# Gathered messages of a graph layer: 18 slots in groups of three, one-hots with one rounded weight, and the weight's rest added to the low halves

## The reference

```python
def _rgcn_conv(x, src, dst, etype, W, root, b):
    x_src = x[src]
    seg = dst * num_rel + etype
    sums = segment_sum(x_src, seg, num_nodes * num_rel)
    cnt = segment_sum(ones, seg, num_nodes * num_rel)
    mean = (sums / maximum(cnt, 1.0)[:, None]).reshape(num_nodes, num_rel, -1)
    out = einsum('nri,rio->no', mean, W)
    return out + x @ root + b

h = relu(_rgcn_conv(xn, src, dst, etype, W1, root1, b1))
gnn = _rgcn_conv(h, src, dst, etype, W2, root2, b2)
x = x + gnn + mix(xn)          # mix: a linear attention
x = x + ffn(_layernorm(x))     # an attention with routed low-rank parts
```

## Time and profile before

| | us |
|---|---|
| median of 3 runs | 3384.78 |
| lowest and highest run | 3378.73, 3389.24 |
| span of the profiled execution | 3605.0 |
| TensorE busy in it | 3193.7 (89%) |
| VectorE | 1792.2 (50%) |
| ScalarE | 782.7 (22%) |
| GpSimd | 1291.1 (36%) |
| layer 0's gather stage, from the 13th gather (636) to the last take (1174) | 538 |
| layer 1's gather stage (1715.5 to 2257.8) | 542 |

### The profile page before, as it was taken

One profiled execution on the slowest core, in us unless ns is written; L12 is line 12 of the kernel. 1 busy time (PEld: TensorE's weight loads), 2 busy tenths in 40 slices (PEclk: granted clock), 3 DMA queues, 4 the chain that ended last, 5 costly groups with the idle time before them and its releaser, 6 DMA issues.

```text
span 3605.0 us, 61984 instructions
## 1 busy us (share of the span) xinstructions
PE 3193.7 (89%) x19397; PEld 2367.7 (66%) x19398; DVE 1792.2 (50%) x2967; ACT 782.7 (22%) x1113; POOL 1291.1 (36%) x1388
## 2 busy tenths in 40 slices
PE   6999999887787799999878878999987899998999
PEld 5788887665665688887666666676755555555555
DVE  6566666444444433333444544334367764556451
ACT  2211211000000312122000000444421345434540
POOL 2681112556555000001555555000042246533652
PEclk9999999989998999999988998999998899999999
DMA  4343344667677133233667767300032000000003
GB/s 142 104 135 118 115 143 132 225 227 251 225 229 232 50 105 113 97 113 115 228 214 237 243 228 227 108 13 26 13 107 70 19 18 18 1 18 18 18 13 104
DMA packets 101161, 433.83 MB, mean 120 GB/s; under 512 B 19648, under 2 KB 19971, under 8 KB 96818
## 3 DMA queue, kind: packets, MB, share of 16 engines
q0 software_dynamic: 55712, 266.87, 22.9%
q1 hardware_dynamic: 42593, 124.83, 11.0%
q10 hardware_dynamic: 2736, 40.50, 3.1%
HBM read 355.21 MB, written 76.88 MB: 120 GB/s over the span
## 4 chain that ended last, share of the span: by engine, by line
PE 64%; DVE 12%; DVEq 7%; issue 7%; another core or an unknown queue 6%; ACT 2%; POOL 1%; DMA 0%; POOLq 0%; ACTq 0%; SPq 0%
PE PS L1574 24%; PE PS L1704 12%; PE PS L1918 5%; PE PS L1737 3%; PE PS L1583 3%; PE PS L1849 2%; DVE NM L1495 2%; DVE HOT L1241 2%; DVEq L1241 2%; PE PS L1745 2%; PE PS L1901 2%; PE PS L1782 1%; PE PS L1902 1%; PE PS L1766 1%
## 5 line engine op out<-in xcount | busy, mean ns | idle before, releaser
L1574 PE MATMUL PS<-WHL,XT 128*125 (+1 forms) x3240 | 553.1, 330 | 13.3 <-DVE WHL L1002 4.2
L1574 PE MATMUL PS<-WHL,HT 128*125 (+1 forms) x3240 | 534.8, 327 | 8.6 <-DVE ROOT L1200 8.6
L1574 PEld LDWEIGHTS PS<-WHL,XT 128*125 128x125 f16 (+1 forms) x3240 | 442.0, 138 | 100.4 <-issue 12.4
L1574 PEld LDWEIGHTS PS<-WHL,HT 128*125 (+1 forms) x3240 | 443.1, 137 | 94.1 <-DVE ROOT L1200 9.0
L1223 DVE SCALAR_TENSOR_TENSOR ROOT<-PS,GS,ROOT x182 | 185.3, 1018 | 523.9 <-remote 257.4
L646 POOL TENSOR_TENSOR PL<-PF 125x500 bf16<-125x500 f32 (+1 forms) x360 | 322.3, 928 | 248.9 <-ACT PF L859 248.2
L1704 PE MATMUL PS<-GATB,HOT 128*125 128x384 f16 x1440 | 285.5, 358 | 94.7 <-DVE HOT L1241 68.3
L1241 DVE SCALAR_TENSOR_TENSOR HOT<-NODE,DSTF,WHLO (+1 forms) x720 | 297.4, 475 | 78.6 <-issue 69.7
L1084 DVE SCALAR_TENSOR_TENSOR MSG<-PS,MSG 125x768 f16<-125x768 f32 x160 | 153.0, 956 | 360.2 <-ACT MSG L685 358.7
L1704 PEld LDWEIGHTS PS<-GATB,HOT 128*125 x1440 | 212.6, 150 | 165.8 <-issue 118.7
L1704 PE MATMUL PS<-ROW,HOT 128*125 128x384 f16 x1392 | 265.4, 350 | 57.8 <-DVE HOT L1241 45.8
(11 more groups left out here) (291 smaller groups left out, 4444.3 us busy)
## 6 DMA issues: line engine op xcount, KB each, us to landing
msg_table<-MSG SPq DMA_DIRECT2D x160, 336.0 KB
WST<-in_wg_dram ACTq DMA_DIRECT2D x16, 2304.0 KB
WST<-in_wf_dram SPq DMA_DIRECT2D x7, 1536.0 KB
KROW<-key_rows POOLq DMA_DIRECT2D x54, 192.0 KB, 3.8
msg_table<-MSG SPq DMA_DIRECT2D x160, 39.0 KB
WST<-in_wm_dram SPq DMA_DIRECT2D x5, 1152.0 KB
GATB<-msg_table,SKEY POOLq DMA_INDIRECT x216
ROW<-msg_table,SKEY POOLq DMA_INDIRECT x216
```

Source lines behind the costliest of these rows:

```text
L1574: ins = pe.matmul(PS[0:ROWS, b0 + h, 0:HALF], X[:, xp, k, bass.ts(t, ROWS)], panel_part(slot, wp, k, h), start=k == 0 and xp + wp == 0, st ...
```

## The change

Groups have three tiles for four, and there are six groups in 18 slots: GATA 6, GATR 4, MSG 2, and GATW 6, which is the weight buffer WST. So layer L has 108 groups, 18 turns of six. HOT holds one f16 number per edge, 128 columns for 125: the weight rounded to f16. It is made by a tensor_scalar (is_equal, then times WSUM). What the rounding leaves is brought in on the other side: `inverse_weights` makes WDEV, the rest of the weight relative to the rounded one; ScalarE writes TMP = WDEV x high half for each tile (128 x 768 f16, signal `shift_made`); VectorE adds TMP to the low halves of a group (3 x 768 f16 in one tensor_tensor, in two for the group that lies across GATR and MSG, signal `lo_made`). TensorE makes two products per tile, 12 matmuls a pass, and waits for `lo_made` in place of the gather itself. WHLO and its two GpSimd operations go. LIM is loaded for three groups at a time.

Since WST is a slot buffer, GpSimd waits before gather 12 (STAGED) for the split of the root panel's successor (`w_lo`), the steps of that panel move to root rows 0, 2, 3 and 4, both layers have five root rows before the passes and the others after turns 0, 3, 6, 9 and 12 of 18, and three loads are put later: the panel after (to after `rows_done`), the second layer's bias (likewise), and the second part of the mix weight (after `rows_done` 2, ahead of the `gnn_rows` stores).

```diff
-AT = 4
+AT = 3
 AG = TILES // AT
-GSETS = 3
+GSETS = 6
+LPACK = 3
+TURNS = AG // GSETS
...
+STAGED = 4 * AT
-ROOT_AT = (((0, 5), (5, 6), (10, 7), (15, 8), (20, 9)), ((0, 3), (3, 4), (7, 5), (11, 6), (15, 7), (19, 8), (23, 9)))
+ROOT_AT = (((0, 5), (3, 6), (6, 7), (9, 8), (12, 9)), ((0, 5), (3, 6), (6, 7), (9, 8), (12, 9)))
...
+        def low_runs(gg):
+            runs = {2: ((GATR, 0, 0, 3),), 3: ((GATR, 3, 0, 1), (MSG, 0, 1, 2))}.get(gg)
+            return runs or ((GATA, gg * AT, 0, 3) if gg < 2 else (GATW, gg * AT - STAGED, 0, 3),)
...
-                sp.wait_ge(*((S["bias_free"], 1) if L == 0 else (S["root_made"], RT)))
+                sp.wait_ge(*((S["bias_free"], 1) if L == 0 else (S["rows_done"], 1)))
...
             sp.wait_ge(S["w_lo"], W_MIX + 1)
+            sp.wait_ge(S["rows_done"], 2)
             sp.dma_start(WST[:, 0:WM], a["wm"][128:256, :]).then_inc(S["w_in"], 16)
-            sp.wait_ge(S["rows_done"], 2)
...
-                g.tensor_copy(WHLO[:, :, 0], WSUM[:])
-                g.drain()
-                g.tensor_tensor(WHLO[:, :, 1], WSUM[:], WHLO[:, :, 0], ALU.subtract)
-                g.drain()
...
-                    if L == 0 and t == GSLOTS:
-                        edge_weights(0)
+                    if t == STAGED:
+                        if L == 0:
+                            edge_weights(0)
+                        g.wait_ge(S["w_lo"], (REL + 1) * (L + 1) + 1)
+                        g.sem_inc(S["pool_tick"], 1)
...
+                act.wait_ge(S["inverse_made"], 1)
+                act.wait_ge(S["root_made"], RT * (L + 1))
+                with act.Fori(0, TURNS) as i:
+                    for gg in range(GSETS):
+                        act.wait_ge(S["lo_made"], i * GSETS + (AG * L + gg + 1))
+                        for k in range(AT):
+                            slot = gg * AT + k
+                            act.wait_ge(S[f"gat_in{slot}"], i * 16 + (16 * TURNS * L + 16))
+                            act.activation(TMP[:, gg % 2, k, :], gat_slot(slot)[:, 0:D], ACT.Copy,
+                                           scale=WDEV[:, bass.ds(i * GSLOTS + slot, 1)]).then_inc(S["shift_made"], 1)
...
-                v.reciprocal(WALL[:], WALL[:]).then_inc(S["inverse_made"], 1)
+                v.reciprocal(WALL[:], WALL[:])
+                v.drain()
+                v.wait_ge(S["root_made"], RT)
+                v.tensor_scalar(TMP[:, 0, 0, 0:TILES], WALL[:, 0:TILES], W_TOP, None, ALU.mult)
+                v.drain()
+                v.scalar_tensor_tensor(WDEV[:], WALL[:, 0:TILES], W_TOP, TMP[:, 0, 0, 0:TILES], ALU.mult, ALU.subtract)
+                v.drain()
+                v.tensor_scalar(WALL[:, 0:TILES], TMP[:, 0, 0, 0:TILES], 1.0 / W_TOP, None, ALU.mult)
+                v.drain()
+                v.reciprocal(TMPF[:], WALL[:, 0:TILES])
+                v.drain()
+                v.scalar_tensor_tensor(WDEV[:], WDEV[:], 1.0 / W_TOP, TMPF[:], ALU.mult, ALU.mult).then_inc(S["inverse_made"], 1)
...
-                    if t == 1:
+                    if t == 0:
                         panel_max(nq, ncols)
+                    elif t == 2:
+                        top_row(nq)
                     elif t == 3:
-                        top_row(nq)
-                    elif t == 5:
                         scales(nq)
-                    elif t == 7:
+                    elif t == 4:
                         split_low(nq, WHL if L == 0 else WHM, ncols)
...
+                            v.wait_ge(S["shift_made"], i * GSLOTS + (TILES * L + (gg + 1) * AT))
+                            for buf, at, k, m in low_runs(gg):
+                                ins = v.tensor_tensor(buf[:, at:at + m, D:2 * D], buf[:, at:at + m, D:2 * D], TMP[:, gg % 2, k:k + m, :], ALU.add)
+                            ins.then_inc(S["lo_made"], 1)
...
-                                    v.scalar_tensor_tensor(hot, node, DSTF[:, bass.ds(t, 1)], weight, ALU.is_equal, ALU.mult).then_inc(S["hot_made"], 1)
+                                    v.tensor_scalar(hot, NODE[:, bass.ds(b * NODES, NODES)], DSTF[:, bass.ds(t, 1)], WSUM[:, bass.ds(t, 1)],
+                                                    ALU.is_equal, ALU.mult).then_inc(S["hot_made"], 1)
...
+                                pe.wait_ge(S["lo_made"], i * GSETS + (AG * L + gg + 3))
                                 for k in range(AT):
                                     slot = gg * AT + k
                                     pe.wait_ge(S["hot_made"], n * AT + (k + 1))
-                                    pe.wait_ge(S[f"gat_in{slot}"], i * 16 + (16 * (AG // GSETS) * L + 16))
-                                    for hp, mp in ((0, 0), (0, 1), (1, 0)):
+                                    for mp in range(2):
                                         for h in range(2):
```

More of the change, by code:

```diff
@@ L117, in graph_and_attentions_kernel @@
         GATR = ROWS4[:].bitcast(f16)
+        GATW = WST[:].bitcast(f16).rearrange("p (k c) -> p k c", c=2 * D)
         IDF = sb(top, "IDF", [128, 128], f32)
@@ L138, in graph_and_attentions_kernel @@
         cctx.close()
[L139 to L143, removed]
+        GATA = sb(gctx, "GATA", [128, 2 * AT, 2 * D], f16)
+        HOT = sb(gctx, "HOT", [128, 2 * AT, NODES], f16)
+        bctx = ExitStack()
+        BIAS = sb(bctx, "BIAS", [ROWS, D], f32)
+        bctx.close()
+        TMP = sb(gctx, "TMP", [128, 2, AT, D], f16)
         SKEY = sb(gctx, "SKEY", [128, TILES], i32)
@@ L223, in graph_and_attentions_kernel @@
             hot1_made hot1_used cnt_done hir_made hir_out key_in0 key_in1 key_in2 key_in3 key_in4 keys_ready low_made relations_made relation_in inverse_made rows2_in keys_made counts_found counts_taken
-            hot_made gat_in0 gat_in1 gat_in2 gat_in3 gat_in4 gat_in5 gat_in6 gat_in7 gat_in8 gat_in9 gat_in10 gat_in11 pass_done pass_out group_used weights_made msg_hi rows_done
+            hot_made gat_in0 gat_in1 gat_in2 gat_in3 gat_in4 gat_in5 gat_in6 gat_in7 gat_in8 gat_in9 gat_in10 gat_in11 gat_in12 gat_in13 gat_in14 gat_in15 gat_in16 gat_in17 shift_made lo_made pass_done pass_out group_used weights_made msg_hi rows_done
             rows_top rows_row rows_all act_tick sp_tick pe_tick pool_tick relu_made h_scale h_t h_hi h_free gnn_out
@@ L868, in _ @@
             for n_, k_ in (("acc_done", 1), ("pair_out", 2), ("msg_free", 2), ("bias_free", 1),
[L869 removed]
+                           ("pass_done", 1), ("pass_out", 2), ("lo_made", 2), ("counts_taken", 1), ("h_free", 1), ("mix_act", mix.size["act"]), ("mix_dve", mix.size["dve"]), ("mp_free", 2),
                            ("lg_free", 2), ("ffn_dve", ffn.size["dve"]), ("ffn_act", ffn.size["act"]), ("av_done", PARTED), ("row_in", 16),
@@ L1252, in _ @@
                     first = i + 1
-                passes(first, AG // GSETS)
+                passes(first, TURNS)
                 v.drain()
@@ L1691, in passes @@
                     with pe.Fori(first, end) as i:
-                        limits = set_limits(pe, i)
                         for gg in range(GSETS):
+                            if gg % LPACK == 0:
+                                limits = set_limits(pe, i * (GSETS // LPACK) + gg // LPACK)
                             lo, hi = group_blocks(limits, gg)
@@ L1718, in _ @@
                         ins.then_inc(S["pass_done"], 1)
-                    passes(i, ROOT_AT[L][n_ + 1][0] if n_ + 1 < len(ROOT_AT[L]) else AG // GSETS)
+                    passes(i, ROOT_AT[L][n_ + 1][0] if n_ + 1 < len(ROOT_AT[L]) else TURNS)
             pe.wait_ge(S["rows_done"], 2)
@@ L1946, in lay_out @@
     o["dstG"] = edges(a["dst"], PAD_DST).reshape(AG, AT * 128)
-    o["node"] = np.tile(np.arange(N, dtype=np.float16), (128, 1))
+    nodes = np.full((RT, NODES), -1.0, np.float16)
+    nodes[:, 0:ROWS] = np.arange(N).reshape(RT, ROWS)
+    o["node"] = np.tile(nodes.reshape(-1), (128, 1))
     slots = [edges(a[key], fill, SLOTS * SLOT).reshape(SLOTS, SLOT * 128) for key, fill in (("dst", PAD_DST), ("edge_type_8", 0))]
```

42 lines of the change are left out of this document (21 added, 21 removed).

## The result

| | before | after |
|---|---|---|
| median of 4 runs, us | 3385.77 | 3461.41 |
| lowest and highest | 3378.73, 3389.24 | 3457.69, 3465.34 |
| ratio, 95% interval | | 1.0225, 1.0210 to 1.0239 |

The change makes the kernel 75.6 us slower. The forecast was slower by 113.

The account below looks back on a forecast made before the run. In runs the gather stages go nearly at GpSimd's issue pace; after the change VectorE, 486 us a stage, sets their end, just over GpSimd's 469. Layer 0 +55 and layer 1 +58 on 3384.78 give 3498 us, range 3310 to 3600.

Parts of the forecast that it names:

- GpSimd's waits of 131 and 144 us: Gather stages before: waits taken as longer under the profiler, mostly absent in runs, so stages of about 433 and 427 us.
- GpSimd's term: Gather stages after: 390 us of issue, 68 of delays beside adds, 11 for the rest: 469 us, between 410 and 540.
- VectorE's term: Gather stages after: 4.07 us a group of three, with second passes and root rows 486 us, between 410 and 620.
- the limits: VectorE's loads of limits at L321, for each three groups: 0.38 us a group in its chain.
- TensorE's relief: Gather passes: 12 matmuls for 24, 128 us less work a layer, costed at nothing because it lies beside GpSimd's issue.
- ScalarE's copies: Three copies of 768 columns a group, 0.83 us each, hidden with a double buffered TMP.
- The start: Before the passes: layer 0's 13th gather near 636.5, first one-hot about 637.7; layer 1 +4 us.
- The moved loads: Root panel, BIAS and W_mix's second part loaded later: 0 to 2 us if not covered, taken as 0.
- A: Rival, chance 0.22: GpSimd's stops are in runs too and 18 slots make them fewer, -49 us a layer: 3291 us.
- B: Rival, chance 0.08: VectorE's add runs at one element a cycle, 2.6 us for 1.36, +190 us a layer: 3760 us.
- C: Rival, chance 0.10: gathers aren't held by tensor_tensor; VectorE's small steps run closer, 3.3 us a group: 3400 us.

Follow-up runs that it names:

- the first experiment: The kernel before, unchanged, profiled once more (also the repeated profile): 3598.7 us, span 3596.8.
- The maximum: Changed kernel with VectorE's add replaced by a tensor_reduce maximum over 420 columns of each tile, one SBUF input: 3600.1 us, 1.0016 of the kernel before.
- the one-input one-hots: Kernel before with each one-hot pair made by two tensor_scalar operations in place of one scalar_tensor_tensor: 3607.3 us, 1.0046 of the kernel before.
- the adds by tile: Changed kernel with a group's add as three tensor_tensor of 768 columns: 3605.3 us, 0.9963 of the kernel before.
- the kernel with no rest: Changed kernel without ScalarE's copies and VectorE's add, TensorE waiting for the gathers again: 3555.3 us, 0.9899 of the kernel before.

## Why the prediction was right, and where it was not

**What bounds the stage: right for the runs that decide, for a reason that was half wrong.** I took GpSimd's waits of 131 and 144 us to be mostly absent in runs. There they are: the stages before must have lasted 3385.8 less the 2524.7 us that the profile has outside them (3605.0 - 538.0 - 542.3), 861 together, where I had 433 + 427 = 860. With the 2529.5 us that the repeated profile has outside them it is 856. This is worked out, since no trace of the kernel before without stops exists. But the ground that I gave, that the waits are longer under the profiler, fell with the first experiment. Whether they are there depends on the chip or its condition, and on all three chips of the experiments they were. So the reasoning reached the right stages by a wrong step, and that the sign came out as forecast is in part luck: where the stops are, the change was faster, which I had given 0.24.

**GpSimd's term: right, and the one that set the stage.** I had 390 + 68 + 11 = 469. Measured are 392 (312 x 1.257), 61.9 or 64.8, and 11.8: 465.9 and 469.7. A hold of 0.65 us for each of 104 adds became 0.60 and 0.62. The maximum (no excess) and the one-input one-hots (0.993 to 0.951 us) show it to be the second SBUF input; the adds by tile (under a third of the excess) show that it lasts as long as the one operation. The inference of the Trainium skill ("SBUF — State Buffer", who interferes with whom) that tensor_tensor doesn't hold descriptor generation is not borne out for these gathers: the one behind the add of 650.54 took 1.97 us. They read their row numbers from SBUF (SKEY), and a transfer that reads none wasn't run. Without holds GpSimd would need 404 us, and VectorE would set the stages: less its waits, 53 and 48 us, they'd be about 413 and 421, an estimate, and the change a small gain.

**VectorE's term: the mis-sized one.** I had 4.07 us a group and 486 a stage, and let VectorE set the end. It took 3.53. The add was right (1.36 forecast, 1.358 measured), but not by its working: 0.52 ns an element isn't twice what KTR takes: (0.420 - 0.15)/768 is 0.35 ns, doubled 0.70, and with that the add would have been 1.77 us. The one-hots were 0.31 apart for 0.27. Too much were the limits, 0.38 a group, whose loads hide behind the running operation, take to add (0.93 for 1.10) and add to one-hots (1.27 for 1.36); one-hots to take was 0.10 too little. With 469 in place of 486 the stages give 34 us less, 3464 for 3498, against 3461 measured. The estimate from the Trainium skill ("VectorE: DVE Perf Modes", the perf-mode tier table), 1.38 us, agrees with the measured 1.358.

**TensorE's relief: nothing, as costed**, where signals are on time, by the trace: GpSimd hardly stops, and takes wait for matmuls 19.1 us in all. No run took a product away alone there. With late signals the third product's removal was worth 50 us.

**ScalarE's copies: hidden**, 0.935 us each for 0.83. VectorE waits 80.0 us for them, but ScalarE waits 311.4 us for gathers to land, so it is the data that is late, not ScalarE.

**The start: 3 to 4 us better than said.** Layer 0's 13th gather starts at 633.75 (636.5 forecast), its first one-hot at 634.12 (637.7). In layer 1 the first one-hot came 28.4 us after the first gather, 30 forecast. The moved loads cost nothing: ScalarE's wait in the mix stage is 8.61 us for 8.62, with the load ahead of it.

**Rivals.** A's mechanism exists where stops exist: fewer stops with 18 slots (49.0 us for 197.2 with twelve), and the change faster. Its size was 94 us and is 38, since the holds of 73.5 us a layer cost more than I gave them and since late signals keep the copies and VectorE's longer series in part on the path (45 us, the kernel with no rest). B fell, by the add's 1.358 us. C's first half fell with the held gathers; its second half came true in part: the limits are hidden and a group takes 3.53 us, under C's 3.6, though the one-hots stayed 0.31 apart. With GpSimd held it had no effect but to leave the end to GpSimd.

What stays open: why the kernel before takes 3385 us in one place and 3595 to 3613 on three chips, what in closely spaced gathers slows TensorE's and VectorE's issue and the signals there, and at which spacing it ends. The held gathers' price in time was measured by no run without stops; there it is the accounting of the trace, 61.9 + 64.8 us on an engine that hardly waits.

## What to carry to other kernels

When GpSimd issues gathers and is at the limit, each VectorE operation with two SBUF inputs costs it the rest of that operation, so the length of each counts, not their sum: shorter operations lessen the hold, and one input takes it away. That this also saves time no run here showed, for all of them met stops. Before a waiting time in one profiled execution is left out or counted, compare the span with the time of that very execution, and profile the kernel before once more: the same change was 2.2% slower where gathers ran free and 1.1% faster where they met stops. Where an engine alternates between holds and stops, taking one away gave its time to the other here, three times.

## What the runs showed of the hardware

- An indirect DMA's issue takes 0.957 us and up to 2.14 behind a VectorE tensor_tensor on 2304 f16 elements a partition; a tensor_reduce of 1.46 us or three tensor_scalar of 128 elements beside it leave it at 0.951.
- A tensor_tensor on f16 in SBUF takes 1.358 us for 2304 elements a partition, 0.951 for 1536 and 0.553 for 768.
- With a drain of GpSimd between two indirect DMAs it stands about 3.5 us before the second; a memset of 0.12 us between two adds nearly nothing.
- On three chips signals of finished passes came late, many by 3 to 6 us, while gathers followed each other at 1.26 us. On one of them TensorE's matmuls were seen to start 1.4 us apart, the time was the same at 233 GB/s as at 118, and with gathers 4.7 us apart no signal was late. In the profile of 3461 us none was late at 1.26 us either.
